# A graph layer and a routed expert layer on one core: another order for the first three pairs, with part of their norms on GpSimd

## The chip, the cores and the metric

The kernel runs on one core of a Trainium2 chip. A core has five engines that run side by side, each through its own list of instructions in order: TensorE (PE in the profile), VectorE (DVE), ScalarE (ACT), GpSimd (POOL) and SyncE (SP). They wait for one another by semaphores. Transfers are issued from the lists of SP, ACT and POOL. The metric is the device time of one execution in microseconds (us).

## The reference

32 graphs of 256 nodes with 128 features go through two layers, each on a layer norm of `x` and each added to `x`:

```python
# layer 1, per graph, on layernorm(x)
h = x @ W.T + b
att = sigmoid((h @ a1)[:, :, None] + (h @ a2)[:, None, :] + att_b) * adj * mask_i * mask_j
x = x + (att / (sum(att) + 1e-8)) @ h * mask
# layer 2, per token, on xn = layernorm(x)
topk_vals, topk_idx = top_k(xn @ gate_w + gate_b, 2)        # 2 of 16 experts
moe = sum_k softmax(topk_vals)_k * (relu(xn @ w1[e_k] + b1[e_k]) @ w2[e_k] + b2[e_k])
x = x + layernorm(xn + moe) * gamma + beta
```

All tensors are float32.

## The kernel before

The work is in three stages.

**The graph stage** takes the graphs in 16 pairs (0 to 15), four tiles of 128 rows each. For pair i: `norm1(i)` on ACT, `transpose_x`, `transpose_adj`, `project`, `project_s1` on PE, `keep_h`, `transposed`, `sigmoids` on ACT, four `attend` on DVE (mask and adjacency into `att`), `aggregate` on PE, `residual` and `variance` on DVE (the new x and its mean and variance), then the inverse deviation: on DVE a chain of twelve tiny dependent operations (`half_bits`, `first_guess`, three rounds of `square`, `times_variance`, `better_guess`) and `shift2`. After it come `norm2` on ACT, `transpose_x2` and `gate` on PE, and the routing on DVE: `largest`, `which`, `one_hot`, `choose`, then `rank` on PE, then `row_numbers`, `pick`, `place`. `place` gives the rows of the sorted list in HBM, and POOL sends the pair's tokens there with 8 indirect DMAs (`scatter`, L454). POOL may start pair i when `rows_done` and `xrow_done` have both reached i+1.

Each engine runs a prologue for pairs 0 to 2, written out call by call, and then a loop of `turn(m)`, which mixes stages of neighbouring pairs: on DVE `turn(m)` is residual(m-1), variance(m-1) with the four attends of pair m set between their short operations ("woven"), then the norm chain of pair m-1 mixed with the routing of pair m-2. `rows` of pair m-2 are written at the end of `turn(m)`.

The mean and variance of the input x are taken by DVE (`stats_of(c)`, one call for a chunk of 4 or 8 tiles; 9 chunks, chunk 0 for pair 0, 1 for pair 1, then two pairs each). POOL makes the inverse deviations of chunks 0 to 4 (`rstd1_of` there, two short operations, a `pow` and a product), DVE those of chunks 5, 6 and 7, 8 (`rstd1_of(5)`, `rstd1_of(7)` on DVE). `setup_b2` on DVE waits for the product `centre_b2` of PE, which stands behind `transpose_x(1)` there.

**The expert stage** runs 94 units: a unit is one block of 256 tokens (two tiles) or 128 (one tile) of one expert. The first 16 units have two tiles each. For a unit PE does `turn_x`, `layer1`, `layer2`; ACT issues the loads of the next weights (`load_w1`, at first two a unit), in units 1 to 8 also one `fill`, and does `relu`; DVE does `unit_x` and `unit_y`, and at some units one `add_beta`; POOL does `send`: one indirect DMA for each tile (L477, 143 in all). All engines start the stage where their list for the graph stage ends. SP loads units 16 and up only when all scatters have landed.

**The last stage** reads the two results of every token, adds them, takes the norm and stores.

Loading: SP issues x chunks 3 to 8, and then for each pair `load_w2` and `load_adj`.

Of the kernel before, what the change touches and what calls it, by code (L numbers as in the profile page):

```python
# [119 lines left out]
def build(nc, x, adj, nodemask, gnn_w, gnn_cols, gnn_row, gate_w, gate_b, w1, w2, b1, b2, gamma, beta, out):  # L120
    ctx = ExitStack()
    with ctx:
# [149 lines left out]
        x_kept = sem("x_kept")  # L272
# [43 lines left out]
        def _(sp):  # L316
# [93 lines left out]
        def _(pool):  # L410
# [27 lines left out]

            def rstd1_of(c):
# [3 lines left out]
                g.tensor_scalar(rs1[:, lo:hi], mv1[:, lo:hi, 1], EPS, None, ALU.add).then_inc(pool_step, 1)  # L443
                g.tensor_scalar(shift1[:, 0, lo:hi], mv1[:, lo:hi, 0], -1.0, None, ALU.mult).then_inc(pool_step, 1)
                pool.wait_ge(pool_step, 3 + 3 * c + 2)
                g.tensor_tensor(rstd1[:, lo:hi], rs1[:, lo:hi], neg_half[:, 0:hi - lo], ALU.pow).then_inc(pool_step, 1)
                pool.wait_ge(pool_step, 3 + 3 * c + 3)
# [46 lines left out]
        def _(act):  # L494
# [196 lines left out]
        def _(dve):  # L691
# [120 lines left out]
            def variance(i, weave=()):  # L812
# [10 lines left out]
                dve.sem_inc(dve_passed, 1)  # L823
                for t in range(TPP):
# [3 lines left out]
                dve.wait_ge(dve_step, n)  # L828
                return step(v.tensor_scalar(var_eps[:, :], mv2[:, :, 1], EPS, -0.5, ALU.add, ALU.mult))
# [308 lines left out]
            for u in range(UNITS + 2):  # L1138
                if u == 2:
                    unit_y(0)  # L1140
                if u < UNITS:
                    unit_x(u)
                if u >= 3:
# [13 lines left out]
                if u % 3 == 2 and u // 3 < GROUPS:  # L1157
                    add_beta(u // 3)
# [18 lines left out]
        def _(pe):  # L1177
# [263 lines left out]
```

## Time and profile before

| | us |
|---|---|
| median of 3 runs | 445.52 (445.52 to 446.57) |
| the profiled execution | 446.86 |
| its span | 445.1 |
| busy: PE / DVE / ACT / POOL | 352.3 / 298.6 / 228.6 / 303.1 |
| share of the span | 79% / 67% / 51% / 68% |

No engine is busy all the time, and the shares are averages over three stages. The stages are told apart by time: the graph stage runs from 0 to about 192 us, the expert stage from there to about 400 us, the last stage to the end. A span of an indirect DMA on POOL is followed by 0.30 us in which POOL counts as idle though nothing is waited for.

### The profile page before, as it was taken

To read this page: it belongs to the slowest core of one execution; us is meant where nothing else is said; L and a number is where in the kernel's file an instruction comes from. 1 tells how busy PE (TensorE), PEld (TensorE's weight loads), DVE (VectorE), ACT (ScalarE), POOL (GpSimd) and SP (SyncE) were. 2 spreads that over 40 slices of the span, in tenths; PEclk is the share of its full clock that TensorE was granted. 3 is DMA by queue.
4 is the path that set the end of the run, shared out by engine and by line. 5 is a ranking of instruction groups with operands and counts; after the bars stand their busy time and mean duration, and the time that the engine had idled before them with its cause. 6 is when DMAs were issued, how large, how long until landed. Compare 5 with 4: busy or idle time off the path is not lost.

```text
span 445.1 us, 11219 instructions
## 1 busy us (share of the span) xinstructions
PE 352.3 (79%) x2285; PEld 283.3 (64%) x2285; DVE 298.6 (67%) x1484; ACT 228.6 (51%) x704; POOL 303.1 (68%) x331
## 2 busy tenths in 40 slices
PE   3597868878787766365979988888888898989892
PEld 3476767767686656344758777777777777844330
DVE  4687899999999997347557666575555555621564
ACT  3558969987899764312234333333333333422662
POOL 5620676777777777777777777777777757770565
PEclk9889989998999995559899999999999999999997
DMA  8822445645554574977677677677777767418984
GB/s 243 289 60 72 133 166 147 219 164 163 177 168 159 172 243 131 320 233 233 189 217 212 171 217 214 200 228 223 210 225 218 214 195 203 115 38 293 394 305 141
DMA packets 61683, 88.10 MB, mean 198 GB/s; under 512 B 10213, under 2 KB 40859, under 8 KB 61490
## 3 DMA queue, kind: packets, MB, share of 16 engines
q1 hardware_dynamic: 30786, 43.45, 33.3%
q0 software_dynamic: 10720, 25.32, 15.9%
q10 hardware_dynamic: 20112, 18.63, 13.9%
q8 instruction: 21, 0.34, 0.3%
q14 instruction: 44, 0.36, 0.3%
HBM read 55.61 MB, written 32.73 MB: 198 GB/s over the span
## 4 chain that ended last, share of the span: by engine, by line
PE 24%; DVE 22%; ACTq 21%; issue 12%; ACT 8%; DMA 3%; POOL 1%; DVEq 0%; POOLq 0%
PE psum L1363 7%; ACTq L311 6%; ACTq L632 6%; ACTq L312 6%; ACT hid L637 4%; PE psum L1352 4%; DMA out_dram<-xrow 3%; PE psum L1265 2%; ACT xn L567 2%; DVE i L885 2%; DVE xmid L805 2%; PE psum L1401 2%; PE psum L1402 2%; PE psum L1255 1%; DVE st L819 1%
## 5 line engine op out<-in xcount | busy, mean ns | idle before, releaser
L477 POOL DMA_INDIRECT token_y<-yb,xb x143 | 143.2, 1001 | 47.0 <-issue 35.1
L454 POOL DMA_INDIRECT sorted_x<-xrow,rows x128 | 123.7, 967 | 60.3 <-issue 56.0
L637 ACT ACTIVATE hid<-psum,b_sb 128x256 f32<-128x256 f32 (+1 forms) x188 | 69.6, 420 | 131.1 <-PE psum L1363 59.4
L1363 PE MATMUL psum<-w_sb,hid 128*128 x572 | 85.0, 286 | 14.0 <-ACT hid L637 13.6
L1363 PEld LDWEIGHTS psum<-w_sb,hid 128*128 128x128 f32 x572 | 74.8, 193 | 26.2 <-issue 22.8
L1352 PE MATMUL psum<-xbT,w_sb 128*128 128x256 f32 (+1 forms) x376 | 84.7, 349 | 4.7 <-DVE xbT L1111 2.9
L1120 DVE TENSOR_TENSOR yb<-psum,b_bc 128x256 f32<-128x256 f32 (+1 forms) x94 | 33.9, 361 | 71.7 <-PE psum L1363 68.5
L1352 PEld LDWEIGHTS psum<-xbT,w_sb 128*128 128x128 f32 x376 | 58.4, 194 | 12.6 <-DVE xbT L1111 9.0
L1125 DVE SCALAR_TENSOR_TENSOR yb<-yb,xb 128x128 f32<-128x128 f32 x143 | 46.0, 350 | 3.3
L1247 PE MATMUL psum<-h_sb,att 128*128 128x129 f32 x256 | 37.6, 302 | 10.0 <-DVE att L759 10.0
L1247 PEld LDWEIGHTS psum<-h_sb,att 128*128 128x128 f32 x256 | 34.5, 213 | 12.4 <-issue 9.6
L1342 PE MATMUL psum<-ident_aug,xb 128*128 128x128 f32 x143 | 32.9, 288 | 6.5 <-issue 5.0
L1111 DVE COPY xbT<-psum 128x256 f32<-128x256 f32 (+1 forms) x94 | 33.2, 354 | 5.6 <-PE psum L1342 5.6
L488 POOL TENSOR_TENSOR xrow<-xrow,xmid 128x512 f32<-128x512 f32 x16 | 20.2, 1266 | 21.1 <-DVE xrow L1169 21.1
L567 ACT ACTIVATE xn<-xmid,rs 128x128 f32<-128x128 f32 x64 | 26.3, 482 | 10.1 <-DVE rs L858 9.8
L557 ACT ACTIVATE sig<-psum,h_sb 128x256 f32<-128x256 f32 x64 | 26.2, 479 | 9.9 <-DVE att L759 8.6
L759 DVE SCALAR_TENSOR_TENSOR att<-psum,mask_t,sig 128x256 f32<-128x256 f32 x64 | 29.4, 471 | 0.9 <-PE psum L1216 0.9
L663 ACT ACTIVATE squares<-psum 128x128 f32<-128x128 f32 x64 | 16.7, 310 | 24.5 <-PE psum L1402 24.5
L507 ACT ACTIVATE xn<-xmid,shift,rstd 128x128 f32<-128x128 f32 x64 | 26.4, 486 | 4.5 <-POOL shift L448 4.5
L1255 PE MATMUL psum<-ident_aug,xn 128*128 128x128 f32 x64 | 11.5, 307 | 21.5 <-ACT xn L567 21.4
L1228 PEld LDWEIGHTS psum<-w_aug,xnT 128*128 128x128 f32 x128 | 19.1, 203 | 13.4 <-issue 5.9
L1342 PEld LDWEIGHTS psum<-ident_aug,xb 128*128 128x128 f32 x143 | 17.8, 144 | 13.1 <-issue 12.4
(178 smaller groups left out, 575.6 us busy)
## 6 DMA issues: line engine op xcount, KB each, us to landing
xb<-sorted_x SPq DMA_DIRECT2D x49, 258.0 KB, 2.9
w_sb<-w_dram ACTq DMA_DIRECT2D x94, 128.0 KB, 2.6
adj_in<-adj_dram SPq DMA_DIRECT2D x32, 256.0 KB
got<-token_y SPq DMA_DIRECT2D x16, 512.0 KB, 6.4
xb<-sorted_x SPq DMA_DIRECT2D x45, 129.0 KB, 2.5
out_dram<-xrow ACTq DMA_DIRECT2D x16, 256.0 KB, 3.6
xmid<-x_dram SPq DMA_DIRECT2D x6, 512.0 KB, 7.8
token_y<-yb,xb POOLq DMA_INDIRECT x143
```

The source lines that it names most:

```text
L454: pool.indirect_dma_start(sorted_x, bass.IndirectOffsetOnAxis(ap=rows[:, slot, t, k:k + 1], axis=0), xrow[:, slot, k, t, :], None).then_in ...
L477: pool.indirect_dma_start(token_y, bass.IndirectOffsetOnAxis(ap=xb[:, q, t, TO:TO + 1].bitcast(I32), axis=0), yb[:, h, t, :], None, bounds ...
L567: last = act.activation(xn2[:, t, :], xmid[:, bass.ds(i * TPP + t, 1), :].rearrange("p a c -> p (a c)"), ACT.Identity, bias=rs2[:, 1, t:t ...
L637: last = act.activation(hid[:, u % RING, c, 0:n], psum[:, 2 + u % 2, c * BT:c * BT + n], ACT.Relu, bias=b1_sb[:, c, e])
L759: last = v.scalar_tensor_tensor(out=att[:, p, t, :], in0=adjT_ps[:, p, t * NODES:(t + 1) * NODES], scalar=mask_t[:, (2 * i + p) * TPG + t: ...
L1111: v.tensor_copy(xbT[:, u % RING, 0:n], psum[:, u % 2, 0:n]).then_inc(xbT_done, 1)
L1120: s = step(v.tensor_tensor(yb[:, h, 0:n, :], psum[:, 4 + u % 2, 0:n * D].rearrange("p (t c) -> p t c", c=D), b2_bc[:, e, :].broadcast_to([ ...
L1125: last = v.scalar_tensor_tensor(out=yb[:, h, t, :], in0=yb[:, h, t, :], scalar=xb[:, q, t, WEIGHT:WEIGHT + 1], in1=xb[:, q, t, RES:RES + D ...
L1247: last = mm(agg_v[:, p, it, :], att[:, p, jt, it * P:(it + 1) * P], h_sb[:, slot, p, jt, 0:D + 1], start=(jt == 0), stop=(jt == TPG - 1))
L1342: last = tr(psum[:, u % 2, t * P:(t + 1) * P], xb[:, q, t, 0:D], ident[:, :])
L1352: last = mm(psum[:, 2 + u % 2, c * BT:c * BT + n], w1_sb[:, u % IN_RING, c * P:(c + 1) * P], xbT[:, u % RING, 0:n], start=True, stop=True)
L1363: last = mm(psum[:, 4 + u % 2, t * D:(t + 1) * D], hid[:, u % RING, c, t * P:(t + 1) * P], w2_sb[:, e, c * D:(c + 1) * D].rearrange("p a c ...
```

## The change

Five things are changed.

1. The prologues of PE, ACT and DVE are written in another order. On DVE `stats_of(3)` comes before the attends of pair 0, `setup_b2` and `setup_gate` come later, and the attends of pairs 1 and 2 are woven into residual and variance of pairs 0 and 1. `centre_b2` moves behind `transpose_x(2)` on PE, `project(1, 0)` and `project_s1(1)` ahead of `aggregate(0)`.
2. For pairs 0 and 1 the twelve small operations on DVE are gone. DVE signals `var2_done`, and POOL does `rstd2_of(i)`: two short operations, a `pow`, a product. Both stand ahead of POOL's first scatter.
3. `stats_of(5)` to `stats_of(8)` and both `rstd1_of` of DVE come later (chunk 5 after turn 4, chunk 6 with `rstd1_of(5)` after turn 5, chunks 7 and 8 after turns 7 and 8, `rstd1_of(7)` after turn 9).
4. SP issues `load_w2(2)`, `load_adj(1)`, `load_w2(3)`, `load_adj(2)` ahead of the small store that waits for `setup_b2`. POOL clears its three residual slots before its first `rstd1_of`.
5. In the expert stage `layer2(1)` and `unit_y(1)` stand one unit earlier, `add_beta(k)` six units later.

```diff
@@ SP
+            for e in range(2, 4):
+                load_w2(e, e % 2)
+                load_adj(e - 1)
             sp.wait_ge(b2_ready, 1)
             sp.dma_start(b2_even, b2_less).then_inc(b2_kept, 16)
-            with sp.Fori(1, PAIRS // 2) as j:
+            with sp.Fori(2, PAIRS // 2) as j:
@@ POOL
+            def rstd2_of(i):
+
+                pool.wait_ge(var2_done, i + 1)
+                step(g.tensor_scalar(var2[:, i, 0, :], mv2[:, :, 1], EPS, None, ALU.add))
+                n = step(g.tensor_scalar(var2[:, i, 1, :], mv2[:, :, 0], -1.0, None, ALU.mult))
+                if i:
+                    pool.wait_ge(xn2_done, i)
+                pool.wait_ge(pool_step, n)
+                n = step(g.tensor_tensor(rs2[:, 0, :], var2[:, i, 0, :], neg_half[:, 0:TPP], ALU.pow))
+                pool.wait_ge(pool_step, n)
+                g.tensor_tensor(rs2[:, 1, :], var2[:, i, 1, :], rs2[:, 0, :], ALU.mult).then_inc(rstd2_done, 1)
...
-            for c in range(POOL_X):
+            for slot in range(XROWS):
+                clear_residuals(slot)
+            for c in range(POOL_X - 1):
                 rstd1_of(c)
-                if c < XROWS:
-                    clear_residuals(c)
+            rstd2_of(0)
+            rstd1_of(POOL_X - 1)
+            rstd2_of(1)
@@ ACT
-            norm2(0)
-            transposed2(0)
             for p in range(2):
                 keep_h(2, p, 0)
                 sigmoids(2, p, 0)
+            norm2(0)
             transposed(3)
+            transposed2(0)
+            keep_h(3, 0, 1)
             keep(0)
-            keep_h(3, 0, 1)
             norm1(4)
+            weigh(0)
+            norm2(1)
             keep_h(3, 1, 1)
+            transposed(4)
...
@@ DVE
+                if by_pool:
+                    dve.sem_inc(var2_done, 1)
+                    return n
...
-            setup_b2()
-            setup_gate()
             stats_of(3)
             attend_all(0)
+            residual(0, graphs(1, 0))
+            variance(0, graphs(1, 1), True)
+            setup_b2()
+            setup_gate()
             stats_of(4)
-            residual(0)
-            norm(variance(0))
-            attend_all(1)
-            stats_of(5)
-            residual(1)
-            r = variance(1)
-            attend_all(2)
-            norm_route_and_place(r, 0)
-            turn(3)
-            stats_of(6)
-            rstd1_of(5)
-            for m in range(4, PAIRS + 1):
+            residual(1, graphs(2, 0))
+            variance(1, graphs(2, 1), True)
+            choose(one_hot(which(0, largest(0))))
+            place(0, pick(row_numbers(0)))
+            for m in range(3, PAIRS + 1):
                 turn(m)
-                if m in (6, 7):
+                if m in (4, 5):
                     stats_of(m + 1)
-                if m == 8:
+                if m == 5:
+                    rstd1_of(5)
+                if m in (7, 8):
+                    stats_of(m)
+                if m == 9:
                     rstd1_of(7)
...
-                if u == 2:
-                    unit_y(0)
+                if u in (2, 3):
+                    unit_y(u - 2)
...
-                if u % 3 == 2 and u // 3 < GROUPS:
-                    add_beta(u // 3)
+                if u % 3 == 2 and 0 <= u // 3 - 2 < GROUPS:
+                    add_beta(u // 3 - 2)
```

On TensorE this is the order from the first tiles of pair 0's projections to the first aggregation. L1206 and L1238 are `transpose_x`, L1228, L1231 and L1260, L1263 `project`, L1237 and L1269 `project_s1`, L1197 `centre_b2`, L1247 and L1279 `aggregate`, L1216 and L1248 `transpose_adj`. Before:

```order
13 L1206 MATMUL psum<-ident_aug,xn 128x128 x4
14 L1197 MATMUL psum<-hid 16x128
15 L1247 MATMUL psum<-h_sb,att 128x129 x8
16 L1228 MATMUL psum<-w_aug,xnT 128x130 x2
17 L1231 MATMUL psum<-hid,w_sb 128x128
18 L1237 MATMUL psum<-xnT,u_bc 128x512
```

The same place of the changed kernel:

```order
13 L1238 MATMUL psum<-ident_aug,xn 128x128 x4
14 L1260 MATMUL psum<-w_aug,xnT 128x130 x2
15 L1263 MATMUL psum<-hid,w_sb 128x128
16 L1269 MATMUL psum<-xnT,u_bc 128x512
17 L1279 MATMUL psum<-h_sb,att 128x129 x8
18 L1248 MATMUL psum<-ident_aug,adj_in 128x128 x8
```

The product that `setup_b2` waits for has gone from here, and pair 1's first projection and its `project_s1` now stand ahead of the aggregation of pair 0.

On VectorE this is the stretch from the second chunk of statistics to the end of pair 0's variance. L747/L750 and L774/L777 are `stats_of`, L730 and L735 the two setups, L759 and L786 `attend`, L793 and L820 the start of `residual`, L825 and L855 the end of `variance`. Before, cut at the first of the small operations:

```order
20 L750 BN_AGGR mv<-st 128x2 x8
21 L730 COPY hid<-psum 16x128
22 L735 TENSOR_TENSOR gate_aug<-gate_w_sb,gate_last 128x16
23 L737 SCALAR_TENSOR_TENSOR gate_aug<-gate_b_bc,ident_aug,gate_aug 128x16
24 L747 BN_STATS st<-xmid 128x6 x8
25 L750 BN_AGGR mv<-st 128x2 x8
26 L759 SCALAR_TENSOR_TENSOR att<-psum,mask_t,sig 128x256 x4
27 L747 BN_STATS st<-xmid 128x6 x8
28 L750 BN_AGGR mv<-st 128x2 x8
29 L793 TENSOR_TENSOR den<-psum,mask_t 128x4
```

The same place of the changed kernel:

```order
20 L777 BN_AGGR mv<-st 128x2 x8
21 L774 BN_STATS st<-xmid 128x6 x8
22 L777 BN_AGGR mv<-st 128x2 x8
23 L786 SCALAR_TENSOR_TENSOR att<-psum,mask_t,sig 128x256 x4
24 L820 TENSOR_TENSOR den<-psum,mask_t 128x4
25 L822 TENSOR_SCALAR den<-den 128x4
26 L824 RECIPROCAL den<-den 128x4
27 L786 SCALAR_TENSOR_TENSOR att<-psum,mask_t,sig 128x256
28 L828 TENSOR_TENSOR den<-den,mask_sq 128x4
29 L832 SCALAR_TENSOR_TENSOR xmid<-psum,den,xmid 128x128 x4
```

One chunk of statistics and the two setups no longer stand between the second chunk and the residual of pair 0, and the attends of pair 1 stand inside that residual.

On GpSimd this is what stands between the last `rstd1_of` but one and the first scatter of the changed kernel (L466 to L473 are `rstd2_of`, L455 to L460 `rstd1_of(4)`, L478 the scatters); before, the scatters came right behind `rstd1_of(4)`:

```order
41 L466 TENSOR_SCALAR var<-mv 128x4
42 L467 TENSOR_SCALAR var<-mv 128x4
43 L471 TENSOR_TENSOR rs<-var,neg_half 128x4
44 L473 TENSOR_TENSOR rs<-var,rs 128x4
45 L455 TENSOR_SCALAR rs<-mv 128x8
46 L456 TENSOR_SCALAR shift<-mv 128x8
47 L458 TENSOR_TENSOR rstd<-rs,neg_half 128x8
48 L460 TENSOR_TENSOR shift<-shift,rstd 128x8
49 L466 TENSOR_SCALAR var<-mv 128x4
50 L467 TENSOR_SCALAR var<-mv 128x4
51 L471 TENSOR_TENSOR rs<-var,neg_half 128x4
52 L473 TENSOR_TENSOR rs<-var,rs 128x4
```

## Rows read from the trace of the kernel before

**Rows 1.** Timeline, POOL, first scatters: start us, us, engine, line, what [idle before <-releaser].

```profile
46.10 1.24 POOL L454 DMA_INDIRECT sorted_x<-xrow,rows  x1 [20.05 <-issue]
...
68.12 0.95 POOL L454 DMA_INDIRECT sorted_x<-xrow,rows  x1 [1.84 <-DVE rows L786]
...
88.33 0.96 POOL L454 DMA_INDIRECT sorted_x<-xrow,rows  x1 [0.30 <-issue]
```

**Rows 2.** Timeline, POOL, the first send of unit 9.

```profile
233.99 0.98 POOL L477 DMA_INDIRECT token_y<-yb,xb  x1 [0.62 <-issue]
```

**Rows 3.** Timeline, DVE, results of units 8 and 9.

```profile
229.33 0.61 DVE L1125 SCALAR_TENSOR_TENSOR yb<-yb,xb 128x128 f32<-128x128 f32 x2
...
232.52 0.61 DVE L1125 SCALAR_TENSOR_TENSOR yb<-yb,xb 128x128 f32<-128x128 f32 x2
```

**Rows 4.** Timeline, ACT, first loads of expert weights.

```profile
191.82 3.93 ACTq L312 DMA_DIRECT2D w_sb<-w_dram  x4
```

**Rows 5.** Timeline, DVE, last rows of the graph stage.

```profile
191.96 0.29 DVE L786 TENSOR_REDUCE rows<-picked 128x8 int32<-128x128 f32 x1
```

**Rows 6.** Timeline, DVE, 16 to 20 us.

```profile
16.66 0.28 DVE L730 COPY hid<-psum 16x128 f32<-16x128 f32 x1 [3.50 <-PE psum L1197]
...
17.21 1.64 DVE L747 BATCH_NORM_STATS2 st<-xmid 128x6 f32<-128x128 f32 x8
...
19.44 1.63 DVE L759 SCALAR_TENSOR_TENSOR att<-psum,mask_t,sig 128x256 f32<-128x256 f32 x4
```

**Rows 7.** Timeline, ACT, sigmoids of pair 0 and transposed x of pair 1.

```profile
16.48 0.84 ACT L557 ACTIVATE sig<-psum,h_sb 128x256 f32<-128x256 f32 x2
17.21 0.59 ACT L540 COPY xnT<-psum 127x512 f32<-127x512 f32 x1
```

**Rows 8.** Timeline, PE, aggregations of pairs 0 and 1.

```profile
20.43 3.78 PE L1247 MATMUL psum<-h_sb,att 128*128 128x129 f32 x16 [3.81 <-DVE att L759]
...
31.26 2.02 PE L1247 MATMUL psum<-h_sb,att 128*128 128x129 f32 x16
```

**Rows 9.** Windows: us, length, busy of PE, PEld, DVE, ACT, POOL (instructions), granted clock, DMA share, GB/s.

```profile
15.80:19.20 3.40, 0.83 (x7) 0.38 (x5) 2.47 (x16) 3.28 (x10) 0.66 (x2) 1.00 1.01 320
19.20:26.00 6.80, 5.57 (x23) 5.24 (x24) 5.67 (x33) 0.59 (x3) 4.67 (x8) 0.50 0.25 84
101.10:104.50 3.40, 2.06 (x27) 1.71 (x26) 3.22 (x29) 2.33 (x6) 2.78 (x3) 1.00 0.35 122
104.50:107.90 3.40, 3.31 (x16) 2.91 (x17) 2.99 (x21) 2.75 (x9) 2.49 (x3) 0.51 0.35 115
```

**Rows 10.** Timeline, DVE, rows of pairs 0 to 3, and what stands between.

```profile
44.62 0.28 DVE L786 TENSOR_REDUCE rows<-picked 128x8 int32<-128x128 f32 x1
...
46.37 0.48 DVE L759 SCALAR_TENSOR_TENSOR att<-psum,mask_t,sig 128x256 f32<-128x256 f32 x1 [0.92 <-PE psum L1216]
...
53.83 0.28 DVE L786 TENSOR_REDUCE rows<-picked 128x8 int32<-128x128 f32 x1
54.09 1.64 DVE L747 BATCH_NORM_STATS2 st<-xmid 128x6 f32<-128x128 f32 x8
...
59.15 0.15 DVE L793 TENSOR_TENSOR den<-psum,mask_t 128x4 f32<-128x4 f32 x1
...
63.47 0.26 DVE L829 TENSOR_SCALAR var_eps<-mv 128x4 f32<-128x4 f32 x1
...
67.03 0.28 DVE L786 TENSOR_REDUCE rows<-picked 128x8 int32<-128x128 f32 x1
...
75.82 0.27 DVE L786 TENSOR_REDUCE rows<-picked 128x8 int32<-128x128 f32 x1
```

**Rows 11.** Timeline, POOL, one `rstd1_of` of four columns.

```profile
10.83 0.24 POOL L443 TENSOR_SCALAR rs<-mv 128x4 f32<-128x4 f32 x1 [2.63 <-DVE mv L750]
...
12.58 0.20 POOL L448 TENSOR_TENSOR shift<-shift,rstd 128x4 f32<-128x4 f32 x1
```

**Rows 12.** Costliest groups, ACT: op, out<-in xcount | busy, mean ns | idle before.

```profile
L567 ACT ACTIVATE xn<-xmid,rs 128x128 f32<-128x128 f32 x64 | 26.3, 482 | 10.1 <-DVE rs L858 9.8
```

More of the change, by code:

```diff
@@ L191, in build @@
         newton1 = sb("newton1", [P, 4, 2 * TPX])
+        var2 = sb("var2", [P, 2, 2, TPP])
         lead = sb("lead", [P, TPP])
@@ L437, in clear_residuals, with step @@
                 g.memset(xrow[:, slot, 1, :, RES:RES + D], 0.0).then_inc(res_clear, 1)
+            steps = [3]
+            def step(instruction):
+                instruction.then_inc(pool_step, 1)
+                steps[0] = steps[0] + 1
+                return steps[0]
             def rstd1_of(c):
@@ L442, in rstd1_of @@
                 pool.wait_ge(stats1, c + 1)
[L443 to L447, printed above, removed]
+                step(g.tensor_scalar(rs1[:, lo:hi], mv1[:, lo:hi, 1], EPS, None, ALU.add))
+                n = step(g.tensor_scalar(shift1[:, 0, lo:hi], mv1[:, lo:hi, 0], -1.0, None, ALU.mult))
+                pool.wait_ge(pool_step, n)
+                n = step(g.tensor_tensor(rstd1[:, lo:hi], rs1[:, lo:hi], neg_half[:, 0:hi - lo], ALU.pow))
+                pool.wait_ge(pool_step, n)
                 g.tensor_tensor(shift1[:, 1, lo:hi], shift1[:, 0, lo:hi], rstd1[:, lo:hi], ALU.mult
                                 ).then_inc(rstd1_done, (hi - lo) // TPP)
+            def rstd2_of(i):
[4 more added lines that the diff above has]
+                    pool.wait_ge(xn2_done, i)
+                pool.wait_ge(pool_step, n)
+                n = step(g.tensor_tensor(rs2[:, 0, :], var2[:, i, 0, :], neg_half[:, 0:TPP], ALU.pow))
+                pool.wait_ge(pool_step, n)
+                g.tensor_tensor(rs2[:, 1, :], var2[:, i, 1, :], rs2[:, 0, :], ALU.mult).then_inc(rstd2_done, 1)
             def scatter(slot):
@@ L610, in _ @@
                 sigmoids(2, p, 0)
+            norm2(0)
             transposed(3)
+            transposed2(0)
+            keep_h(3, 0, 1)
             keep(0)
-            keep_h(3, 0, 1)
             norm1(4)
+            weigh(0)
+            norm2(1)
             keep_h(3, 1, 1)
+            transposed(4)
             for p in range(2):
                 sigmoids(3, p, 1)
-            transposed(4)
-            weigh(0)
-            norm2(1)
             for m in range(3, PAIRS + 2):
@@ L810, in residual, with variance @@
                     attend(*weave[1])
-            def variance(i, weave=()):
+            def variance(i, weave=(), by_pool=False):
                 weave = list(weave)
@@ L823, in variance @@
                 dve.sem_inc(dve_passed, 1)
+                if by_pool and i:
+                    dve.wait_ge(rstd2_done, i)
+                    dve.sem_inc(dve_passed, 1)
                 for t in range(TPP):
@@ L1304, in _ @@
             transpose_x(1)
-            centre_b2()
-            aggregate(0, 0)
             project(1, 0, 1)
             project_s1(1)
+            aggregate(0, 0)
+            transpose_adj(1)
             project(1, 1, 1)
-            transpose_adj(1)
             transpose_x(2)
+            centre_b2()
             project(2, 0, 0)
             project_s1(2)
+            project(2, 1, 0)
             aggregate(1, 1)
-            transpose_x2(0, 3)
-            project(2, 1, 0)
+            transpose_x(3)
             transpose_adj(2)
+            transpose_x2(0, 4)
+            project(3, 0, 1)
             gate(0)
-            transpose_x(3)
-            project(3, 0, 1)
             project_s1(3)
-            project(3, 1, 1)
             aggregate(2, 0)
             rank(0)
+            project(3, 1, 1)
             transpose_x(4)
@@ L1389, in _ @@
                     layer1(u - 1)
-                if u >= 3:
+                if u == 2:
+                    layer2(1, e1)
+                elif u >= 4:
                     layer2(u - 2, e2)
```

8 lines of the change are left out of this document (4 added, 4 removed).

## Prediction

> **What bounds the kernel now.** I read the timeline of GpSimd first, because the table by line gives it two groups of indirect DMAs that fill most of the span. From its first scatter GpSimd hardly stops: from 68.12 to 88.33 us [rows 1] sixteen scatters follow at 1.263 us each, and in the whole rest of the graph stage it stands only once, 1.84 us ahead of pair 2. A turn of the other engines takes 8.8 us where nothing is put in (75.82 less 67.03 [rows 10]), a pair on GpSimd 10.1. So GpSimd falls behind the others, is never starved again there, and goes from the last scatter straight into the sends. By this view alone the end would move with the first scatter, at 46.10.
>
> The second view is the timeline of the expert stage, because there GpSimd has suppliers. One send stands at 233.99, 0.62 instead of the usual 0.30 [rows 2]. The result of unit 8 ends on VectorE at 229.94 and that of unit 9 at 233.13, 3.19 us apart [rows 3], while GpSimd takes two tiles, about 2.6 us by its pace of a scatter [rows 1]. The send of unit 9 starts 0.86 after its result; where a scatter surely waited, it started 0.81 after the rows were written (67.03 and 0.28, then 68.12 [rows 1, 10]). So at unit 9 the slack between the supplying chain (ScalarE's loads and relu, TensorE, VectorE) and GpSimd is spent. That chain doesn't start from GpSimd: ScalarE issues the first expert weights at 191.82 [rows 4], when the last pair is routed (its rows are written at 191.96 [rows 5]). Two clocks run therefore: GpSimd from its first scatter, and the chain from the end of the graph stage. The end moves by the smaller of the two gains. This is the step on which my number rests.
>
> **The first aggregation.** Before, VectorE stands 3.50 us for the product of `centre_b2`, then does the two setups and a chunk of statistics (17.21 to 19.44, 2.23 us) and only then pair 0's attends, 1.63 us, to 21.07 [rows 6]. Without that wait VectorE is free at 13.16 (16.66 less 3.50); the chunk ends at 15.4, and the attends wait for the sigmoids, the last of which ends at 17.32 [rows 7]: they are done near 18.2. The chunk's data must be there at 13.2; before it was read only at 17.21, so this is a condition. TensorE now does pair 1's projection and `project_s1` first: transposed x of pair 1 is there at 17.80 [rows 7], the two take about 1.8 us (an estimate: `sig` and `xnT` of rows 7 take 0.84 and 0.59 for as many columns), and the aggregation starts at 19.6 instead of 20.43 [rows 8]. It took 3.78 us at the granted clock 0.50 [rows 8, 9]; pair 1's took 2.02 at full clock. I take full clock: it ends at 21.5 instead of 24.21.
>
> GpSimd's three clears (now ahead of its first `rstd1_of`) delay pair 0's x by about half a us. I cost this at nothing: ScalarE does pair 1's norm before `keep_h(0)`, and that norm waits for GpSimd until 12.78 [rows 11]. Were that cover gone, it is 0.5.
>
> **Pair 0.** A residual and variance with woven attends is 4.3 us from its first operation to the end of the variance (59.15 to 63.47 [rows 10]). So pair 0's variance is there at 25.8. GpSimd's replacement of the small chain costs what its four-column `rstd1_of` does, 1.95 us (10.83 to 12.78 [rows 11]), and runs beside VectorE. VectorE then has the setups (0.55) and a chunk (2.2), until 28.6. Residual of pair 1 waits for its aggregation. From 21.5 on TensorE has the adjacency and second projection of pair 1 (1.8), then ScalarE copies, does a sigmoid and hands over pair 2's x (0.5, 0.84, 0.59 [rows 7]), to 25.2; TensorE's two projections of pair 2 with `project_s1` and ScalarE's copy between them take 2.9, and the aggregation 2.0 [rows 8]: 30.1. Where I have no row I estimate by those; the sum may be 1 off either way. With 0.6 more for pair 2's adjacency its variance ends at 35.0, and routing of pair 0, now without the other chain mixed in, takes 3.2: rows at 38.2 instead of 44.90 (44.62 and 0.28 [rows 10]). First scatter near 39.2 instead of 46.10: GpSimd gains 6.9.
>
> **Pair 1.** Its norm is now on the path: 35.0 and 1.95 on GpSimd, then four operations of `norm2(1)` on ScalarE, 1.6 (four of 0.48 [rows 12] that overlap a little), copies of about 1.1 ahead of TensorE's projection of pair 4, and with it half of pair 3's adjacency, about 1.5: pair 3's first attend at 41.2. Before, it stood at 46.37 after a wait of 0.92 [rows 10], and rows of pair 1 ended 7.74 later (54.11). Now 41.2 and 7.74 give 48.9: of 6.7 gained, 5.2 are left. `rstd2_of(1)` also stands ahead of the first scatter on GpSimd, but ends at 37.0, before the scatter can start.
>
> **Pairs 2 to 4.** The moved statistics are not free here. Before, from rows 1 to rows 2 were 13.20 us (53.83 to 67.03), of which 5.05 (54.09 to 59.15) were chunk 6 and `rstd1_of(5)`, and the next turn took 8.8 [rows 10]. A turn behind inserted work is thus 8.15, since VectorE no longer waits for the gate. Now turn 4 is plain (8.8), turn 5 follows chunk 5 (8.15 and 2.2) and turn 6 follows chunk 6 and `rstd1_of(5)` (13.2): 32.35 for the three where before 13.2 and twice 8.8 made 30.8. So 1.55 goes back: rows of pair 4 gain 3.65. The later chunks cost the same as before, one turn later. GpSimd reaches pair 4 at 49.7 and three times 10.1, 80.0; the rows end near 81.3 and the scatter starts near 82.1 instead of 88.33 [rows 1]. It stands about 2 us and keeps a gain of 6.2. From there it falls behind again and is not starved.
>
> **Later.** The graph stage ends 3.65 us earlier, unless TensorE's clock falls at other places than before. Its rows wait for scatters three pairs back, which come earlier too. The chain of the expert stage starts 3.65 earlier, and GpSimd, which could be 6.2 earlier, gives up 2.5 at units 3 to 9, where the slack was nil. `layer2(1)` one unit earlier feeds nobody who waits, since the first send starts long after unit 1's result. `add_beta` leaves two early places: its price is bounded by nothing and by four attends (0.48 for 256 columns [rows 10], and it has 512), 1.9 us gained; at unit 9 VectorE gets its inputs 3.19 us apart [rows 3] and has room, so I take 0, and keep the 1.9 for the range. Loads of SP: `load_adj(1)` and (2) are no later than before; cost 0. The last stage follows rigidly. Sum: 3.7 us. The profiled execution, 446.86, would become 443.2 and the median 445.52 would become 441.8 (the profiled execution was 1.34 over that median, and its span 445.1).
>
> **A rule weighed.** The clock fell at 19.2 after a stretch in which TensorE was busy 0.83 of 3.40 us, and it stayed at 0.50, the lower of its levels (1.2 GHz), until 26.0 [rows 9]; it fell again at 104.5 after a stretch with 2.06 busy. The Trainium skill (TensorE: Matmul & The Clock Gate, section HAM oscillation) says that waits between bursts of matmuls throttle the engine again. The trace agrees at 19.2. It also shows a fall with no long wait before it, at 104.5. By the rule the new order, whose longest wait there is 1.5 us, keeps the full clock and gives the 441.8.
>
> **Rivals.**
> 1. *Half clock at the first aggregation after all.* For it: the new order leaves TensorE some 1.9 us busy where 0.83 were, and 2.06 was followed by a fall [rows 9]. Against: a wait of 3.81 [rows 8] is gone. The aggregation takes up to 3.78 instead of 2.02 and its neighbours a little: 1.8 of the gain goes, 443.6.
> 2. *GpSimd is the only bound.* If the slack at unit 9 is larger than I read, or the chain speeds up when results leave sooner, the end follows the first view: 6.2, and 439.3. For it: GpSimd stands there only 0.32 us more than its usual 0.30 [rows 2]. Against: rows 3, a supplier slower than the sends.
> 3. *The start doesn't move.* Chunk 3 or pair 1's adjacency lands late, and VectorE stands with the attends behind it. If the chunk comes only at 17.2, aggregation is as before; the small chain, the weaving and the taken-out wait still give part, less the 1.55: near 444.8, within the noise.
> 4. *Slower.* The place is turn 6 of ScalarE: `norm1(8)` now waits for `rstd1_of(5)`, which ends 5 us after turn 5, and behind it are sigmoids of pair 7, the kept rows of pair 4 and `norm2(5)`; on TensorE the transposes of pair 8 stand ahead of an aggregation and a rank. ScalarE has 5.0, then 1.65 and about 4.9 of other work, 11.6, before `norm2(5)` is wanted at 13.2: hidden by 1.6. It decides only if ScalarE's turn is over 5.3 us longer than I add up (1.6 hidden and 3.7 gained); a second such place (pair 12) doubles what lies beyond. With 7 at the first and 2 at the second it would be about 447.5.
>
> **How the numbers follow.** Forecast 0.52; half clock 0.18; GpSimd alone 0.15; start not moved 0.10; slower 0.05. What a measurement can tell from no change is about 0.3%, 1.3 us, so faster means under 444.2. The forecast has its own range, 440.4 to 443.2: my sums for the pieces of pairs 0 and 1 may be 1.3 off either way. The forecast and GpSimd alone are faster, of half clock about four fifths: 0.82. Same: the rest of half clock and most of start not moved: 0.13. Slower 0.05. The range leaves out the far part of GpSimd alone and of the last two: 438.8 to 444.4.
>
> **What would show it.** Right: the first scatter at 38.5 to 40, the first aggregation near 2 us long, a wait of GpSimd of about 2 us ahead of pair 4's scatters, rows of pair 15 near 188.3, first send near 204, and new waits of GpSimd for VectorE's results in units 3 to 9. Wrong: a first scatter earlier by 6 or more and no new waits at the sends (then rival 2), an aggregation of over 3 us (rival 1), VectorE idle between 13 and 17 us for x (rival 3), ScalarE standing at `norm1(8)` with `norm2(5)` late (rival 4).

## The result and the profile after

| | before | changed |
|---|---|---|
| median, first chip (11 runs each) | 445.52 | 441.69 (440.44 to 444.64) |
| ratio, 95% interval | | 0.9914 [0.9896, 0.9933] |
| median, another chip (11 and 5 runs) | 446.39 | 441.21 (440.44 to 441.86) |
| ratio, 95% interval | | 0.9875 [0.9855, 0.9896] |
| the profiled execution, its span | 446.86, 445.1 | 440.44, 438.7 |

Faster, by 3.8 us on the first chip and 5.2 on the second. The forecast was 441.8. The two profiled executions differ by 6.4, more than the medians, so a place of the trace is compared with the forecast's place, not with the end. Of these 6.4, 6.38 are there at GpSimd's first send; from there to the last send the changed kernel needs 0.95 more than before (189.81 and 188.86), and behind the last send 0.97 less (43.9 and 44.9; in the fourteen traces told of here this stretch takes 43.8 to 45.3).

GpSimd, the timeline, at its first scatter, at pair 4, and at the first send (columns as in [rows 1]):

```profile
39.74 1.22 POOL L478 DMA_INDIRECT sorted_x<-xrow,rows  x1 [2.59 <-DVE rows L813]
...
82.56 0.96 POOL L478 DMA_INDIRECT sorted_x<-xrow,rows  x1 [2.37 <-DVE rows L813]
...
203.97 1.00 POOL L504 DMA_INDIRECT token_y<-yb,xb  x1 [0.30 <-issue]
```

The first scatter is 6.36 us earlier than in [rows 1]. Between its first scatter and the first send, which came at 210.35 before, GpSimd stands once, before pair 4, 2.07 over its usual 0.30. In the first ten units it then stands at four sends, those of units 3, 7, 8 and 9:

```profile
212.12 0.98 POOL L504 DMA_INDIRECT token_y<-yb,xb  x1 [0.65 <-issue]
...
222.64 0.98 POOL L504 DMA_INDIRECT token_y<-yb,xb  x1 [0.53 <-issue]
...
226.19 0.98 POOL L504 DMA_INDIRECT token_y<-yb,xb  x1 [1.28 <-DVE yb L1157]
...
229.14 0.98 POOL L504 DMA_INDIRECT token_y<-yb,xb  x1 [0.68 <-issue]
```

Less 0.30 each, that is 1.94 us, where before there was one such wait of 0.32 [rows 2]. VectorE, its timeline, the rows of pairs 0, 1, 2 and 15, and the first attend of pair 3 (answers to [rows 5, 10]):

```profile
38.48 0.29 DVE L813 TENSOR_REDUCE rows<-picked 128x8 int32<-128x128 f32 x1
...
41.39 0.48 DVE L786 SCALAR_TENSOR_TENSOR att<-psum,mask_t,sig 128x256 f32<-128x256 f32 x1 [2.14 <-PE psum L1248]
...
48.98 0.27 DVE L813 TENSOR_REDUCE rows<-picked 128x8 int32<-128x128 f32 x1
...
57.65 0.28 DVE L813 TENSOR_REDUCE rows<-picked 128x8 int32<-128x128 f32 x1
...
188.41 0.29 DVE L813 TENSOR_REDUCE rows<-picked 128x8 int32<-128x128 f32 x1
```

TensorE's first aggregation, and the two windows of [rows 9] around it (length, busy of PE, PEld, DVE, ACT, POOL, granted clock, DMA share, GB/s):

```profile
19.73 1.95 PE L1279 MATMUL psum<-h_sb,att 128*128 128x129 f32 x16
```

```profile
15.80:19.20 3.40, 1.86 (x14) 1.49 (x14) 1.80 (x5) 3.28 (x10) 2.60 (x6) 1.00 1.10 351
19.20:26.00 6.80, 5.51 (x40) 4.45 (x39) 3.94 (x19) 3.79 (x12) 0.00 (x0) 1.00 0.40 132
```

The clock stayed at its upper level, and the aggregation took 1.95 us where [rows 8] had 3.78.

### The profile page after: what moved, and what is told of

It reads as the page before. It is cut to its first block, busy times and chain, and to the rows that moved or that the text cites. A ratio compares the mean times of both kernels' runs of the same rounds, so it can differ in the third digit from the quotient of the medians.

```text
span 438.7 us, 11187 instructions
## 1 busy us (share of the span) xinstructions
PE 348.4 (79%) x2285; PEld 280.7 (64%) x2285; DVE 294.9 (67%) x1458; ACT 228.6 (52%) x704; POOL 305.5 (70%) x339
## 4 chain that ended last, share of the span: by engine, by line
DVE 25%; PE 25%; ACTq 18%; issue 12%; ACT 9%; DMA 3%; POOL 1%; DVEq 1%; POOLq 0%
PE psum L1395 6%; ACTq L659 6%; ACTq L313 5%; PE psum L1384 5%; ACTq L312 5%; ACT hid L664 4%; ACT xn L594 3%; PE psum L1435 2%; PE psum L1436 2%; DVE i L918 2%; DVE xmid L832 2%; PE psum L1297 2%; DVE st L846 2%; PE psum L1287 2%; DMA out_dram<-xrow 1%
## 5 line engine op out<-in xcount | busy, mean ns | idle before, releaser
L478 POOL DMA_INDIRECT sorted_x<-xrow,rows x128 | 123.2, 962 | 43.4 <-issue 37.2
L1384 PE MATMUL psum<-xbT,w_sb 128*128 128x256 f32 (+1 forms) x376 | 83.5, 345 | 5.7 <-DVE xbT L1143 4.5
L1279 PE MATMUL psum<-h_sb,att 128*128 128x129 f32 x256 | 35.9, 293 | 3.8 <-DVE att L786 3.8
L1279 PEld LDWEIGHTS psum<-h_sb,att 128*128 128x128 f32 x256 | 33.4, 206 | 6.2 <-issue 5.7
L786 DVE SCALAR_TENSOR_TENSOR att<-psum,mask_t,sig 128x256 f32<-128x256 f32 x64 | 30.0, 471 | 3.7 <-PE psum L1248 2.7
L1260 PEld LDWEIGHTS psum<-w_aug,xnT 128*128 128x128 f32 x128 | 18.2, 195 | 12.3 <-issue 5.7
```

The lines of the kernel that those rows point to most:

```text
L478: pool.indirect_dma_start(sorted_x, bass.IndirectOffsetOnAxis(ap=rows[:, slot, t, k:k + 1], axis=0), xrow[:, slot, k, t, :], None).then_in ...
L786: last = v.scalar_tensor_tensor(out=att[:, p, t, :], in0=adjT_ps[:, p, t * NODES:(t + 1) * NODES], scalar=mask_t[:, (2 * i + p) * TPG + t: ...
L1279: last = mm(agg_v[:, p, it, :], att[:, p, jt, it * P:(it + 1) * P], h_sb[:, slot, p, jt, 0:D + 1], start=(jt == 0), stop=(jt == TPG - 1))
L1384: last = mm(psum[:, 2 + u % 2, c * BT:c * BT + n], w1_sb[:, u % IN_RING, c * P:(c + 1) * P], xbT[:, u % RING, 0:n], start=True, stop=True)
```

## The experiments

All start from the changed kernel; all ratios are to the kernel before, in runs on the same chip. The changed kernel itself had 0.9914 and, on another chip, 0.9875, so ratios of different groups can't be compared closer than about 0.4%. Groups: first e1, e2, e7, e3; then e4, e5, e6, e8; then a2, e9, e10, e12. My theory is that of the prediction: the end goes by two clocks, GpSimd's and that of the chain that supplies its sends. The main rival is that GpSimd alone counts. No run takes back the order of SP's loads or the place of `centre_b2` alone, so their shares of the gain are not known.

**Later GpSimd, once a little and once a lot.** In `turn(0)` of POOL:

```diff
                 pool.wait_ge(rows_done, i + 1)
+                if i == 0:
+                    for _ in range(2):      # e7: range(5)
+                        n = step(g.tensor_tensor(idle_t[:, :], ones_f[:, 0:2 * TPP], neg_half[:, :], ALU.pow))
+                        pool.wait_ge(pool_step, n)
```

> The changed kernel, with two idle powers of eight columns (1.67 us each) on GpSimd between the waits of pair 0's turn and its first scatter; nothing else is changed. Two clocks (my theory): the first scatter moves from 39.7 to about 43.2 us; the wait of 2.37 ahead of pair 4 shrinks to its idle 0.30 and takes 2.07 of the 3.4, so the first send moves from 204.0 to 205.3; that is absorbed by the waits for VectorE's results in units 3 to 9. Median 441.7, not above 442.1, ratio to the kernel before about 0.991. GpSimd alone (rival 2 of the prediction): the 1.3 that is left is passed on to the end, 443.0, ratio 0.994. If even the wait at pair 4 were only apparent: 3.4 later, 445.1.

> As the run with two idle powers, but with five (8.35 us) ahead of GpSimd's first scatter. The first scatter moves to 48.1, the first send to 210.3, where the kernel before had it, while the other engines' graph stage stays 3.6 earlier than before. Two clocks: GpSimd is now the later of the two; the waits in units 3 to 9 vanish and take 2.8 of the 6.3, the rest passes: 445.2, ratio 0.999. GpSimd alone: all 6.3 pass, 448.0, ratio 1.006. Supplying chain alone: no change, 441.7.

Measured: e1 442.96, ratio 0.9953 [0.9931, 0.9975]; e7 444.93, ratio 0.9990 [0.9964, 1.0016]. The timelines of GpSimd, e1's powers, its first scatter and first send:

```profile
39.05 3.35 POOL L488 TENSOR_TENSOR idle_t<-ones_f,neg_half 128x8 f32<-128x8 f32 x2 [1.75 <-DVE rows L818]
45.73 1.22 POOL L479 DMA_INDIRECT sorted_x<-xrow,rows  x1 [3.33 <-issue]
...
208.12 1.00 POOL L509 DMA_INDIRECT token_y<-yb,xb  x1 [0.30 <-issue]
```

and e7's first scatter and first send:

```profile
47.97 1.22 POOL L479 DMA_INDIRECT sorted_x<-xrow,rows  x1 [0.99 <-POOL idle_t L488]
...
210.63 1.00 POOL L509 DMA_INDIRECT token_y<-yb,xb  x1 [0.30 <-issue]
```

e1's delay was not 3.4 but 6.0 us: behind the two powers GpSimd stood another 3.33 with nothing named as the cause. Its expectation, 441.7, was for a smaller delay and is thus missed. With the real one GpSimd alone gives, after the 2.07 at pair 4, 3.9 to 4.2 later at the end, 445.6 or more; two clocks take another 1.94 off, 443.7. Measured was 443.0. e7 moved the first send by 6.66, just to where the kernel before has it. The expectation had 448.0 for GpSimd alone and 445.2 for two clocks, measured 444.9. That 445.2 lets the waits of units 3 to 9 take 2.8; with the 1.94 of the changed kernel's trace it would be 446.4. Trace against trace the sum closes: 6.66 less 1.94 is 4.7, and the spans are 443.4 and 438.7; for e1, 4.15 less 1.94 is 2.2, and the spans differ by 1.7. By the ratios e7 is 3.4 us above the changed kernel's first group and 5.1 above its second, each to about 1.5; both are under 6.66, the second only just. In e1 and e7 the waits in units 3 to 9 are gone. So a delay of GpSimd's first send reaches the end only in part: GpSimd alone falls.

**Later chain.** On ACT, ahead of the first loads of expert weights:

```diff
             act.wait_ge(h_g, 2 * PAIRS)
+            for k in range(8):
+                act.activation(idle_t[:, k, :], ones_f[:, 0:14], ACT.Relu)
```

> The changed kernel, with eight idle activations of 14 columns (about 0.23 us each, 1.8 together) on ScalarE between the graph stage and the first loads of expert weights. GpSimd is not touched. Two clocks: the supplying chain starts 1.8 later, GpSimd waits 1.8 more in units 3 to 9, median 443.5, ratio 0.995. GpSimd alone: 0 to 0.3, 441.7, ratio 0.991. The expert stage's own edits as the source of the gain say nothing here.

Measured: 443.07, ratio 0.9949 [0.9927, 0.9971]. The timelines of ScalarE and of VectorE (last rows) show that the eight took half of what I had put in, and where they lie:

```profile
188.39 0.92 ACT L672 ACTIVATE idle_t<-ones_f 128x14 f32<-128x14 f32 x8
189.36 3.83 ACTq L314 DMA_DIRECT2D w_sb<-w_dram  x4
```

```profile
189.53 0.29 DVE L816 TENSOR_REDUCE rows<-picked 128x8 int32<-128x128 f32 x1
```

In this trace the whole graph stage ended 1.12 later than in the changed kernel's (last rows 189.53 and 188.41), so the chain is counted from the last rows. By that count the loads were issued only 0.22 later (0.17 ahead of the rows, where the changed kernel has them 0.39 ahead), and `unit_y` of units 1 and 2 starts 12.73 and 16.36 behind the rows, where the changed kernel's two traces have 12.60 and 16.23, and 12.75 and 16.38. So the delay did not reach the chain, and the rise of the median (ratio higher by 0.0035 than in the first group, with an uncertainty of 0.003) can't be laid to it. GpSimd stood 2.85 us at unit 3 and 0.71 and 0.84 at units 8 and 9; what stands at unit 3 is told below. The number came near the expected 443.5 by luck, and the run says nothing for or against two clocks.

**Relief of the chain, one part at a time.** e3 takes the fills off ScalarE (units 1 to 8), e8 puts TensorE's `table_row`, at which it stands for VectorE's table entries, one unit later:

```diff
@@ e3, SP and ACT
-            for e in range(0, EXPERTS, 2):
+            for e in range(EXPERTS):
...
-                if u == 1:
-                    act.wait_ge(fill_done, 1)
-                if 1 <= u <= EXPERTS // 2:
-                    fill(2 * u - 1)
@@ e8, PE
-                if u == 5:
+                if u == 6:
                     table_row()
```

> The changed kernel, with all sixteen fills of pad rows issued by SyncE and none by ScalarE, which before issued eight of them in units 1 to 8 at about 0.65 us each. GpSimd and the graph stage are not touched. Two clocks: ScalarE's turn in units 1 to 8 falls from 3.2 to about 2.6 us, GpSimd's waits in units 3 to 9 go (1.5 to 2.8 us together), median 439.6, ratio 0.987. GpSimd alone: 0, 441.7, ratio 0.991. A loss could come if SyncE's fills are late for the first token loads that read them: up to 1.

> The changed kernel with TensorE's table_row one unit later (6 instead of 5). In the trace TensorE stands 2.63 us at it for VectorE's table entries, with the layers of units 3 to 5 behind it. Two clocks: the supplying chain gains 2 to 2.6 us from unit 3 on, GpSimd's waits in units 3 to 9 (1.94 over the idle between DMAs) go, median 439.8, ratio 0.987. GpSimd alone: no change, 441.7, ratio 0.991. If the chain only catches up with the next limit (ScalarE with a fill in each of units 1 to 8): half of it, 440.8.

Measured: e3 441.16, ratio 0.9910 [0.9882, 0.9939]; e8 441.71, ratio 0.9901 [0.9878, 0.9925]. Both expectations missed: neither gained anything that can be told. The timelines of GpSimd, from its first send to unit 9, say why. All the waits of e3:

```profile
214.31 0.98 POOL L504 DMA_INDIRECT token_y<-yb,xb  x1 [2.71 <-DVE yb L1153]
```

and of e8 (units 5 to 9):

```profile
218.31 0.98 POOL L504 DMA_INDIRECT token_y<-yb,xb  x1 [0.56 <-issue]
...
221.44 0.98 POOL L504 DMA_INDIRECT token_y<-yb,xb  x1 [0.86 <-DVE yb L1157]
...
224.45 0.98 POOL L504 DMA_INDIRECT token_y<-yb,xb  x1 [0.75 <-issue]
...
227.76 0.98 POOL L504 DMA_INDIRECT token_y<-yb,xb  x1 [1.03 <-DVE yb L1157]
...
230.71 0.98 POOL L504 DMA_INDIRECT token_y<-yb,xb  x1 [0.69 <-issue]
```

Less 0.30 each, 2.41 and 2.39 us: about as much as in the changed kernel (1.94, and 2.57 in its second trace), at other units. With the fills gone the chain stands at the table row (unit 3); behind it the results of units 4 to 7 come 1.97 us apart. With the row moved it is paced by ScalarE, whose relus of units 4 to 9 start 3.05 us apart, and reaches unit 9 as late. Timeline of TensorE in e3, at the row, and the window behind it:

```profile
207.55 0.38 PE L1360 MATMUL psum<-ident_aug,blk 128*1 128x128 f32 x2 [2.55 <-DVE blk L1076]
```

```profile
208.40:211.80 3.40, 3.33 (x13) 3.01 (x14) 0.42 (x1) 0.84 (x2) 2.59 (x3) 0.56 0.88 249
```

Behind that wait the clock fell to its lower level (layer 2 of a unit took 1.91 us for 1.05). This was open, then: two limits of the same height, or no limit at all? Taking both away tells it. Beside it ran the changed kernel again:

> The changed kernel itself, unaltered, beside the next two on one chip, so that small differences are read within one chip. Ratio 0.991 as before.

> The changed kernel with both single edits that brought next to nothing alone: all fills on SyncE, and table_row one unit later. In the first alone the supplying chain stood at the table row (GpSimd waited 2.71 at unit 3), in the second at ScalarE's fills (waits in units 5 to 9, 2.8 over the idle). If the chain is the slower of the two, taking both away ends the waits in units 3 to 9: 1.9 to 2.4 less, 439.5, ratio 0.986. If GpSimd's waits at the sends are not what the end follows (GpSimd alone), or a third limit of the same height stands behind: 441.2 to 441.7, ratio 0.990 to 0.991.

Measured: a2 441.21, 0.9875 [0.9855, 0.9896]; e9 438.41, 0.9812 [0.9790, 0.9834], 1.1 under what I expected. Timelines of GpSimd, the first send, the first of unit 9 and the last one, in a2:

```profile
204.28 1.00 POOL L504 DMA_INDIRECT token_y<-yb,xb  x1 [0.30 <-issue]
...
230.04 0.98 POOL L504 DMA_INDIRECT token_y<-yb,xb  x1 [0.68 <-issue]
...
394.81 0.98 POOL L504 DMA_INDIRECT token_y<-yb,xb  x1 [0.30 <-issue]
```

and in e9:

```profile
205.53 1.00 POOL L504 DMA_INDIRECT token_y<-yb,xb  x1 [0.30 <-issue]
...
228.91 1.42 POOL L504 DMA_INDIRECT token_y<-yb,xb  x1 [0.30 <-DVE yb L1153]
...
392.96 0.98 POOL L504 DMA_INDIRECT token_y<-yb,xb  x1 [0.30 <-issue]
```

In e9 the waits in units 3 to 9 are gone: no send there stands longer than 0.35. The result of unit 9 is written 6.3 us ahead of its send, in a2 0.86. From its first send to its last GpSimd needs 187.43 us, a2 190.53. Nothing of GpSimd or of the graph stage was changed in e9, so the chain did hold the end, and neither of its two limits shows while the other stands. The medians differ by 2.8 us, and a2's waits in units 3 to 9 are 2.57. The two traces differ in more than that, by amounts that nearly cancel: a2 also stands 2.8 longer at its 98th and 114th sends, and e9's sends 19 to 96 take 2.0 longer, both without a known cause.

**The statistics.** In e6 VectorE does chunk 5 while it waits for pair 3's adjacency:

```diff
             place(0, pick(row_numbers(0)))
+            stats_of(5)
             for m in range(3, PAIRS + 1):
                 turn(m)
-                if m in (4, 5):
-                    stats_of(m + 1)
                 if m == 5:
+                    stats_of(6)
                     rstd1_of(5)
```

> The changed kernel with one chunk of statistics (chunk 5, 2.2 us) moved from behind turn 4 to right behind the routing of pair 0, where VectorE stands 2.14 us ahead of pair 3's first attend; chunk 6 stays behind turn 5. My term for pairs 2 to 4 says that the chunk costs 1.5 us net there: rows of pair 4 end at 80.2 instead of 81.8, GpSimd's wait of 2.37 ahead of pair 4 shrinks to about 0.8, the last rows of the graph stage come 1.5 earlier (186.9). Both clocks gain 1.5: 440.2, ratio 0.988. Rival (the graph stage's later turns are paced by something else, such as GpSimd's scatters of pairs before or ScalarE): rows of pair 15 stay at 188.4 and the median at 441.7.

Measured: 440.19, ratio 0.9857 [0.9830, 0.9884], 1.5 us under e8 on the same chip. Timelines of VectorE (rows of pairs 4 and 15) and of GpSimd (first scatter of pair 4):

```profile
79.98 0.27 DVE L813 TENSOR_REDUCE rows<-picked 128x8 int32<-128x128 f32 x1
...
187.02 0.29 DVE L813 TENSOR_REDUCE rows<-picked 128x8 int32<-128x128 f32 x1
```

```profile
81.13 0.96 POOL L478 DMA_INDIRECT sorted_x<-xrow,rows  x1 [0.30 <-issue]
```

Rows of pair 4 come 1.49 earlier and those of pair 15 1.39, though this run's rows of pair 0 were 0.57 late (39.05). The wait ahead of pair 4 is gone. The term "1.55 goes back" of the prediction is confirmed in place and size; the changed kernel's own trace agrees, with 32.49 us from the rows of pair 1 to those of pair 4 (48.98 to 81.47) where the kernel before has 30.84 (53.83 to 84.67).

**Half of the change undone.** e4 keeps the new order but gives the inverse deviations of pairs 0 and 1 back to VectorE:

```diff
@@ POOL
-            rstd2_of(0)
             rstd1_of(POOL_X - 1)
-            rstd2_of(1)
@@ DVE
-            variance(0, graphs(1, 1), True)
+            norm(variance(0, graphs(1, 1)))
...
-            variance(1, graphs(2, 1), True)
-            choose(one_hot(which(0, largest(0))))
-            place(0, pick(row_numbers(0)))
+            norm_route_and_place(variance(1, graphs(2, 1)), 0)
```

> The changed kernel in its new order, but the inverse deviations of pairs 0 and 1 are again made by VectorE's chain of small operations (norm right behind variance 0, the mixed norm and routing behind variance 1), and GpSimd's two rstd2_of are gone. My theory: the small chain of pair 0 lies ahead of the setups and the chunk and delays pair 1's residual, that of pair 1 is mixed with pair 0's routing and delays rows 0; first scatter about 2.5 later (42.2), the graph stage's end 2 to 3 later; both clocks lose, median 444 (443.3 to 444.8), ratio 0.995 to 0.999: over half of the gain hangs on the hand-over to GpSimd. Rival (the order of the prologue alone brings the gain, the hand-over saves only what lay beside waits): 442, ratio 0.992.

Measured: 446.65, ratio 1.0017 [0.9999, 1.0035], more lost than I expected: the whole gain. Timeline of VectorE, rows of pairs 0, 1 and 15:

```profile
39.72 0.28 DVE L811 TENSOR_REDUCE rows<-picked 128x8 int32<-128x128 f32 x1
44.68 0.48 DVE L784 SCALAR_TENSOR_TENSOR att<-psum,mask_t,sig 128x256 f32<-128x256 f32 x1 [4.12 <-PE psum L1244]
...
52.54 0.28 DVE L811 TENSOR_REDUCE rows<-picked 128x8 int32<-128x128 f32 x1
...
191.93 0.29 DVE L811 TENSOR_REDUCE rows<-picked 128x8 int32<-128x128 f32 x1
```

Rows of pair 0 lose only 1.24, those of pair 1 3.56 and those of pair 15 3.52: 191.93, where the kernel before had 191.96 [rows 5]. The price is paid behind pair 1's late norm, where VectorE stands 4.12 us for TensorE instead of 2.14. GpSimd starts at 40.98, 5.12 earlier than before the change, and loses most of that ahead of pairs 1 and 4:

```profile
53.62 0.96 POOL L478 DMA_INDIRECT sorted_x<-xrow,rows  x1 [2.54 <-DVE rows L811]
...
86.25 0.96 POOL L478 DMA_INDIRECT sorted_x<-xrow,rows  x1 [2.60 <-DVE rows L811]
...
208.00 1.00 POOL L502 DMA_INDIRECT token_y<-yb,xb  x1 [0.30 <-issue]
```

Its first send is still 2.35 earlier than before, by which GpSimd alone would give 443.6, ratio 0.995. It then stands at units 3, 8 and 9, 2.7 over the usual idle. That the first send comes 2.35 earlier, the last rows come when they came before, and the end does not move is the plainest case of the two clocks.

**The expert stage's own edits.**

```diff
-                if u in (2, 3):
-                    unit_y(u - 2)
+                if u == 2:
+                    unit_y(0)
...
-                if u % 3 == 2 and 0 <= u // 3 - 2 < GROUPS:
-                    add_beta(u // 3 - 2)
+                if u % 3 == 2 and u // 3 < GROUPS:
+                    add_beta(u // 3)
```

and `layer2(1)` back likewise.

> The changed kernel with the edits of the expert stage undone: layer2(1) and unit_y(1) in their old place, add_beta(k) at unit 3k+2 again. Two clocks with the prediction's value 0 for these edits: 441.7, ratio 0.991. If add_beta in units 2 and 5 (about 1 us of VectorE each) delays the supplying chain where GpSimd now waits (units 3 to 9): up to 1.9 slower, 443.6, ratio 0.995. If these edits were the source of the gain: 445.

Measured: 442.24, ratio 0.9925 [0.9901, 0.9948]: against e8 on the same chip 0.5 slower, less than can be told. These edits don't carry the gain.

**The version that beats both.** e10 is e9 with e6's edit.

> As e9_fills_and_row, and with chunk 5 of the statistics right behind the routing of pair 0. Nothing waits for another then but GpSimd for the first rows: first send 202 to 202.5 (in a run whose first scatter is at 39.7), no waits in units 3 to 9, 2.07 and 1.9 less than the changed kernel: 437.9, ratio 0.983. Without the chain's part it would stay where the run with chunk 5 alone was, 0.986.

Measured: 437.60, ratio 0.9798 [0.9773, 0.9823]: 8.8 us under the kernel before, 3.6 under the changed one on the same chip. The total is what I expected (437.9). Over e9 it gains 0.8, less than the 1.6 expected, and the intervals overlap. First scatter to first send takes 162.60 (40.68 to 203.28) where e9 has 164.38, so GpSimd's part is there.

## Why the prediction was right, point by point

- **First aggregation.** Said: 19.6, full clock, to 21.5. Measured: 19.73 to 21.68. Rival 1 did not come: both windows show 1.00 with 1.86 busy in the first, the value the rival had feared. Rival 3 is out too: VectorE took chunk 3 at 13.53 without standing for it. The clears, which I had costed at nothing, moved the norm of pair 1 from 12.81 to 13.07, 0.26.
- **Pair 0.** Said: rows at 38.2, first scatter 39.2. Measured: rows 38.48 to 38.77, scatter 39.74. The pieces on the way agree too, so the total isn't made of errors that cancel: pair 0's variance 26.12 (said 25.8), the second aggregation's end 30.46 (30.1), pair 1's variance 34.97 (35.0).
- **Pair 1.** Said: first attend of pair 3 at 41.2, rows 48.9, "of 6.7 gained, 5.2 are left". Measured: 41.39 and 48.98 to 49.25. In e4 these rows came 3.56 later, and the whole gain was gone.
- **Pairs 2 to 4.** Said: rows near 81.3, scatter near 82.1, a wait of about 2. Measured: scatter 82.56, wait 2.07. e6 takes the term away and gets it back.
- **The graph stage's end.** Said: 3.65 earlier. Measured: 3.55 (188.41 against 191.96 [rows 5]). Rival 4 would have shown as a late turn behind chunk 6; rows of pair 5 follow 8.8 behind those of pair 4 (90.25 and 81.47).
- **Two clocks.** Said: first send near 204, new waits in units 3 to 9, GpSimd gives up 2.5 there, the end moves by 3.7. Measured: 203.97, 1.94 us at units 3, 7, 8 and 9 (0.32 before, so 1.6 more were given up; in the second trace 2.25), medians 3.8 and 5.2. e7, e4 and e9 support it from three sides, and rival 2 falls with them; e2, meant as a fourth, doesn't count. That 441.8 was met within 0.1 is in part luck: on the other chip the same kernel gained 1.4 more.
- **Where the sum was less right than its total.** I read the chain at unit 9 alone and named ScalarE, TensorE and VectorE as one supplier. It has two limits of the same height, the table row at unit 3 and the fills in units 1 to 8, and only e3 and e8 made me see the first. In the profiled executions the chain gained more than the graph stage did: the result of unit 9 ended 4.85 earlier (228.28 against 233.13 [rows 3]), 1.3 over the 3.55. The lead grows from 3.24 to 4.61 between the results of units 2 and 3, which stand on either side of the table row. Before the change (timeline of VectorE) and after it:

```profile
208.34 0.61 DVE L1125 SCALAR_TENSOR_TENSOR yb<-yb,xb 128x128 f32<-128x128 f32 x2
...
215.26 0.62 DVE L1125 SCALAR_TENSOR_TENSOR yb<-yb,xb 128x128 f32<-128x128 f32 x2
```

```profile
205.10 0.61 DVE L1157 SCALAR_TENSOR_TENSOR yb<-yb,xb 128x128 f32<-128x128 f32 x2
...
210.65 0.61 DVE L1157 SCALAR_TENSOR_TENSOR yb<-yb,xb 128x128 f32<-128x128 f32 x2
```

Before, the clock fell at 210.35 behind the row and came back at 213.8; in the changed kernel's trace it didn't fall. The term was not in my sum. That the clock is also why unit 9 gained is not shown: counted from the last rows, `unit_y` of unit 9 starts at 40.10 before and at 38.80 and 39.43 in the changed kernel's two traces, but also at 39.42, 39.54 and 39.04 in e1, e7 and e12, whose list for TensorE is the changed kernel's and where the clock fell. Nor can I give the clock to the change. It fell near the table row (between 204 and 211 us) in ten of the fourteen traces told of here, in e4 and e8 ahead of the row; it did not in the changed kernel's two, e9 and e10. What decides it stays open.

The Trainium skill (TensorE: Matmul & The Clock Gate, section HAM oscillation) says that waits between bursts of matmuls throttle the engine again. At the table row the traces agree in part. In nine of them TensorE waits 2.52 to 2.63 us there at a granted clock of 1.00. In seven the clock then falls, as in e3 (a wait of 2.55, then 0.56). In the changed kernel's two it does not, with waits of 2.63 and 2.56:

```profile
207.12 0.38 PE L1364 MATMUL psum<-ident_aug,blk 128*1 128x128 f32 x2 [2.63 <-DVE blk L1080]
```

```profile
205.00:208.40 3.40, 1.12 (x8) 0.78 (x9) 1.93 (x12) 0.84 (x2) 2.51 (x3) 1.00 0.56 149
208.40:211.80 3.40, 3.40 (x26) 3.22 (x25) 1.72 (x5) 0.84 (x2) 2.45 (x3) 1.00 0.78 243
```

## What to carry to other kernels

When a busy engine runs back to back through two stages, its early start is worth only as much as its suppliers in the later stage can follow: find the unit where the slack between result and consumer is smallest, and take the smaller gain. If relieving that place brings nothing, look whether the wait only moved to another unit before you drop the theory; two limits of the same height must be removed together (here nothing that can be told from either alone, and 2.8 us from both). Put inserted work where its engine already waits (2.2 us of statistics in a wait of 2.14).

## What was not expected of the hardware

GpSimd stands at its 114th send in every kernel traced, without a supplier that is late (in two traces, those of the kernel before and of a2, also at the 98th, 0.86 and 1.40). In the changed kernel:

```profile
352.50 1.05 POOL L504 DMA_INDIRECT token_y<-yb,xb  x1 [0.30 <-issue]
356.32 0.98 POOL L504 DMA_INDIRECT token_y<-yb,xb  x1 [2.77 <-DVE yb L1157]
```

In the kernel before it was 2.77 at 361.74, 3.4 after the result that it is put down to had been written; elsewhere 0.86 to 2.77. One run asked what it hangs on. It has four indirect DMAs more, between the statistics and `rstd2_of(0)`, whose rows are all out of bounds:

```diff
+            for _ in range(4):
+                pool.indirect_dma_start(
+                    token_y, bass.IndirectOffsetOnAxis(ap=pad_rows[:, TO:TO + 1].bitcast(I32), axis=0),
+                    pad_rows[:, 0:D], None, bounds_check=ITEMS - 1, oob_is_err=False).then_inc(extra, 16)
             rstd2_of(0)
```

> The changed kernel with four indirect DMAs more on GpSimd, issued where it idles between 18.9 and 26 us, that move nothing (all their rows are out of bounds and are dropped). It asks about a stall that all kernels so far show at the same DMA, the 114th send (GpSimd's 242nd indirect DMA), of 0.6 to 2.5 us over the usual idle. If it hangs on the number of indirect DMAs that GpSimd has issued, it comes at the 110th send now; if on the number of rows moved, or on the work of the other engines, at the 114th as before.

The one run took 442.58, and its stall came at the 114th send as before:

```profile
354.09 0.99 POOL L509 DMA_INDIRECT token_y<-yb,xb  x1 [0.31 <-issue]
357.78 0.98 POOL L509 DMA_INDIRECT token_y<-yb,xb  x1 [2.70 <-DVE yb L1162]
```

So, by this one trace, it isn't the number of DMAs issued. What it is stays open; the 3.33 us behind e1's powers may be the same kind of thing. An indirect DMA whose rows are all dropped still took GpSimd 0.97 to 1.24 us, no less than one that moves them.
